# Two joined graph layers on one core: wo's last rows as one packed product, y scaled on ScalarE, and another order of root's low parts

## What is computed

```python
# layer 0 (2 relations, width 286), on norm_x = ln_weight * x * rsqrt(mean(x^2) + eps)
out = norm_x @ W_root + bias + sum_r segment_mean_r(norm_x @ W_rel[r])     # 625 x 286
y   = elu(out) @ wo_weight                                                 # 286 x 1024
x1  = layernorm(x + (x + y))
# layer 1 (8 relations, width 1024)
u   = x1 @ root + bias + sum_r segment_mean_r(x1) @ weight[r]
z   = concat([u, x1]) @ w_gate + b_gate
h   = tanh(u) * z + x1 * (1 - z)
return layernorm(x1 + h)
```

## Time and profile before

| | us |
|---|---|
| median of 3 runs (838.40 to 838.87) | 838.75 |
| the profiled execution's own time | 838.58 |
| its span | 836.8 |
| TensorE busy | 818.8 |
| VectorE (DVE) busy | 671.8 |
| ACT busy | 438.3 |

### The profile page before, as it was taken

How to read it: one execution, slowest core, us unless ns; L and a number is a source line. 1 busy time by engine, 2 the same in 40 slices (tenths; PEclk the granted TensorE clock), 3 DMA queues, 4 the chain that set the end, 5 groups by cost and what they waited for, 6 DMA issues and landing times.

```text
span 836.8 us, 15905 instructions
## 1 busy us (share of the span) xinstructions
PE 818.8 (98%) x6326; PEld 586.4 (70%) x6326; DVE 671.8 (80%) x969; ACT 438.3 (52%) x606; POOL 14.4 (2%) x32
## 2 busy tenths in 40 slices
PE   7999999999999999999999999999999999999996
PEld 6566744468876868768677686786867868768544
DVE  8999698998978677687776777767778677788996
ACT  6888568376555354453554535535446254445711
POOL 1000000000000000000000000000000000000000
PEclk9999999999999999999999999999999999999998
DMA  9512369202220220202202112022020220305711
GB/s 316 114 26 27 131 224 227 101 1 101 102 101 1 101 102 1 100 15 85 100 0 100 44 56 100 0 100 71 29 100 0 100 100 2 127 1 151 201 51 73
DMA packets 60124, 70.82 MB, mean 85 GB/s; under 512 B 30662, under 2 KB 34370, under 8 KB 60083
## 3 DMA queue, kind: packets, MB, share of 16 engines
q1 hardware_dynamic: 59207, 69.39, 26.3%
q10 hardware_dynamic: 876, 0.85, 0.4%
HBM read 57.71 MB, written 5.18 MB: 75 GB/s over the span
## 4 chain that ended last, share of the span: by engine, by line
PE 88%; DVE 7%; ACT 3%; issue 1%; DMA 1%; SPq 0%; DVEq 0%; ACTq 0%
PE psP L1162 51%; PE psA L1233 21%; PE psP L982 12%; PE psA L971 2%; PE psP L1086 1%; PE psP L942 1%; ACT cu_mem L676 1%; DVE p_mem L1463 1%; DVE vec L1384 1%; ACT wsplit L709 1%; DVE p_mem L1462 1%; ACT dump L596 0%; DMA stage<-in_src 0%; DVE wsplit L1410 0%; DMA xT<-cu_mem 0%
## 5 line engine op out<-in xcount | busy, mean ns | idle before, releaser
L1162 PE MATMUL psP<-wsplit,xT 128*128 128x256 f16 x2592 | 294.6, 273 | 0.0
L1162 PEld LDWEIGHTS psP<-wsplit,xT 128*128 128x128 f16 x2592 | 253.6, 98 | 33.0
L1233 PE MATMUL psA<-p_mem,cu_mem 128*128 128x512 f16 x800 | 175.3, 379 | 0.0
L1162 PE MATMUL psP<-wsplit,x 128*128 128x256 f16 x1296 | 150.3, 273 | 0.0
L1233 PEld LDWEIGHTS psA<-p_mem,cu_mem 128*128 (+1 forms) x800 | 78.2, 98 | 91.1 <-DVE cu_mem L1722 0.3
L1162 PEld LDWEIGHTS psP<-wsplit,x 128*128 128x128 f16 x1296 | 126.8, 98 | 14.7
L1424 DVE SCALAR_TENSOR_TENSOR wsplit<-stage,sc,wsplit 128x1024 f16<-128x1024 f32 x90 | 114.8, 1279 | 26.8 <-ACT wsplit L671 26.8
L671 ACT ACTIVATE wsplit<-stage,sc 128x1024 f16<-128x1024 f32 x90 | 100.6, 1137 | 16.6 <-DVE sc L1302 10.6
L1722 DVE SCALAR_TENSOR_TENSOR cu_mem<-psA,coef,cu_mem 128x512 f32<-128x512 f32 x80 | 60.0, 750 | 31.3 <-PE psA L1233 29.9
L671 ACT ACTIVATE wsplit<-x,sc 128x1024 f16<-128x1024 f32 x54 | 61.7, 1143 | 41.6 <-PE psP L1162 31.0
L1424 DVE SCALAR_TENSOR_TENSOR wsplit<-x,sc,wsplit 128x1024 f16<-128x1024 f32 x54 | 69.2, 1282 | 10.2 <-ACT wsplit L671 9.8
(11 more groups left out here) (207 smaller groups left out, 792.5 us busy)
## 6 DMA issues: line engine op xcount, KB each, us to landing
stage<-in_L_gnn_weight SPq DMA_DIRECT2D x16, 2048.0 KB, 7.7
stage<-in_L_gnn_w_gate SPq DMA_DIRECT2D x4, 2048.0 KB, 8.2
x_home<-x SPq DMA_DIRECT2D x5, 512.0 KB, 3.8
x<-x_home SPq DMA_DIRECT2D x5, 512.0 KB, 5.5
x<-in_x SPq DMA_DIRECT2D x4, 512.0 KB, 8.6
xT<-in_L_gnn_root SPq DMA_DIRECT2D x1, 2048.0 KB, 8.9
stage<-in_L_gnn_root SPq DMA_DIRECT2D x1, 2048.0 KB, 8.4
out<-x SPq DMA_DIRECT2D x4, 512.0 KB
```

The lines of the kernel that those rows point to most:

```text
L1162: last = nc.tensor.matmul(psP[:, bank, (col + tt) * FB:(col + tt + 1) * FB], lhs[tt](a, c), split_block(n, b)[:, c, :], start=(first and t ...
L1233: last = nc.tensor.matmul(psA[:, (NT * h + t) % 2, :], cnt8[:, r, s, t * P:(t + 1) * P], p_part[h][a][:, s, :], start=(s == 0 and a == 0), ...
```

## The change

- wo's last 30 rows are loaded three times, at partitions 0, 32 and 64 of the last chunk. y's last 30 columns are also written three times, so that after the turn partitions 0 to 29, 32 to 61 and 64 to 93 of the last chunk hold them. wo's rows at partitions 32 to 63 are replaced by their low part, y's columns at partitions 64 to 95 by theirs. One matmul over 96 partitions then gives all three products (`packed_product`), 7 matmuls instead of 9 per half tile.
- `wo_high` and `wo_low` go chunk by chunk, `wo_low` right behind `first_sums` on DVE and no longer behind `agg0_add(3)`; `unit_scale(U_WO)` goes ahead of the last `first_sums`. TensorE asks for the last `q_done` only at the ninth matmul of the aggregates.
- y is scaled on ACT (`y_scaled`: two activations with a scale and a bias a tile), with the bias from one tiny DVE operation (`y_shift`). The parts of root's `weight_sum` and of `raw_high(U_ROOT)` are placed anew around it.
- `y_low` becomes two operations, 256 columns on all partitions and 128 columns on partitions 64 to 95.
- All four low parts of root's first half come before the first `wo_add`. `y_high(4)` comes behind the first deviation on ACT.
- `aggregate0(4)` goes ahead of `turn_y(0)` and `turn_y(1)`. wo's products 7 and 8 go to the two banks of `psA`, 9 to bank 2 of `psP`, and root's products 2 to 4 wait for all ten adds of wo.

```diff
@@ sync
-            sp.dma_start(st_wo[0:F - (FC - 1) * P, FC - 1, :], wo_d[(FC - 1) * P:F, :]).then_inc(wo_tail_loaded, 16)
+            for q in range(3):
+                sp.dma_start(st_wo[q * QUAD:q * QUAD + FREST, FC - 1, :], wo_d[(FC - 1) * P:F, :]).then_inc(wo_tail_loaded, 16)
-            sp.wait_ge(wo_lo, 1)
+            sp.wait_ge(wo_lo, FC)
             load(U_ROOT + 1, 1, by_chunk(root_d[:, HALF:D]))
@@ scalar
+            def y_scaled(t):
+                act.wait_ge(y_factors, 1 if t < 2 else 2)
+                last = elu_tmp[:, t, F - FREST:F].unsqueeze(1).broadcast_to([P, 2, FREST])
+                twice = acc0[:, t, F - FREST + QUAD:F - FREST + 3 * QUAD].rearrange("p (q f) -> p q f", q=2)[:, :, 0:FREST]
+                nc.scalar.activation(twice, last, ACT.Identity, bias=y_shift[:, t:t + 1], scale=rows_f[:, 0, 2, t:t + 1])
+                nc.scalar.activation(acc0[:, t, 0:F], elu_tmp[:, t, :], ACT.Identity, bias=y_shift[:, t:t + 1],
+                                     scale=rows_f[:, 0, 2, t:t + 1]).then_inc(y_ready, 1)
-            for t in range(NT - 1):
-                elu_exponential(t)
-            y_high(0)
-            y_high(1)
-            weight_sum(U_ROOT, 0, slot_load(U_ROOT), parts=(0, 1))
-            elu_exponential(NT - 1)
-            weight_sum(U_ROOT, 0, slot_load(U_ROOT), parts=(2, 3))
+            elu_exponential(0)
+            elu_exponential(1)
+            weight_sum(U_ROOT, 0, slot_load(U_ROOT), parts=(0,))
+            y_scaled(0)
+            y_scaled(1)
+            weight_sum(U_ROOT, 0, slot_load(U_ROOT), parts=(1, 2, 3))
+            elu_exponential(2)
+            elu_exponential(3)
+            y_high(0)
+            elu_exponential(NT - 1)
+            y_high(1)
+            raw_high(U_ROOT, 0, (0, 1, 2))
+            for t in range(2, NT):
+                y_scaled(t)
             y_high(2)
             y_high(3)
-            raw_high(U_ROOT, 0)
-            y_high(4)
+            raw_high(U_ROOT, 0, (3,))
...
             for t in range(NT):
                 ln_deviation(0, t)
+                if t == 0:
+                    y_high(NT - 1)
                 x1_apply(t)
@@ tensor
+            def packed_product(out, t, cols):
+                _, hi, lo = unit_weights(U_WO)
+                for c in range(FC - 1):
+                    for a, w, first in ((0, hi, c == 0), (0, lo, False), (1, hi, False)):
+                        nc.tensor.matmul(out, yT[:, a, c, bass.ts(t, P)], w[:, c, cols], start=first, stop=False)
+                return nc.tensor.matmul(out, yT[0:3 * QUAD, 0, FC - 1, bass.ts(t, P)], hi[0:3 * QUAD, FC - 1, cols],
+                                        start=False, stop=True)
-                pe.wait_ge(wo_added, NT + t + 1)
+                pe.wait_ge(wo_added, NT + t + 1 if t < 2 else 2 * NT)
+            WO_FREE = {NT: (wo_added, 1), NT + 1: (wo_added, 2), NT + 2: (y_lo, 4), NT + 3: (y_lo, 5), NT + 4: (wo_added, 3)}
@@ vector
+            def wo_low(c):
+                st, hi, lo = (v[:, c, :] for v in unit_weights(U_WO))
+                if c == FC - 1:
+                    st, hi, lo = (v[QUAD:2 * QUAD, :] for v in (st, hi, hi))
+                dve.wait_ge(wo_hi, c + 1)
+                scale = sc_f[QUAD:2 * QUAD, scale_col(U_WO, 1), 2:3] if c == FC - 1 else sc_f[:, scale_col(U_WO, 1), 2:3]
+                stt(lo, st, scale, hi, ALU.mult, ALU.subtract).then_inc(wo_lo, 1)
...
+            unit_scale(U_WO, 1)
             dve.wait_ge(flag_ready, 1)
...
             first_sums(NT - 1, 1)
...
-            unit_scale(U_WO, 1)
+            for c in range(FC):
+                wo_low(c)
...
+            def y_factor(t0, t1):
+                tiles = slice(t0, t1)
                 dve.wait_ge(elu_done, t1)
+                step(nc.vector.tensor_reduce(rowmax[:, 0, tiles], elu_tmp[:, tiles, :], AX.X, ALU.max))
+                row_scales([rows[:, 0, a, tiles] for a in range(4)], rowmax[:, 0, tiles].bitcast(I32), least=127)
+                ts(y_shift[:, tiles], rows_f[:, 0, 2, tiles], -1.0, None, ALU.mult).then_inc(y_factors, 1)
+                ts(cy[:, tiles], rows_f[:, 0, 3, tiles], sc_f[:, U_WO, 3:4], 0.5, ALU.mult, ALU.mult).then_inc(cy_ready, 1)
             def y_low(t):
                 dve.wait_ge(y_hi, t + 1)
+                nodes, third = slice(t * P, (t + 1) * P), slice(2 * QUAD, 3 * QUAD)
+                tt(yT[:, 1, 0:FC - 1, nodes], psA[:, t % 2, 0:FPAD - P].rearrange("p (c n) -> p c n", c=FC - 1),
+                   yT[:, 0, 0:FC - 1, nodes], ALU.subtract)
+                tt(yT[third, 0, FC - 1, nodes], psA[third, t % 2, FPAD - P:FPAD], yT[third, 0, FC - 1, nodes],
+                   ALU.subtract).then_inc(y_lo, 1)
             agg0_add(0)
             agg0_add(1)
-            elu_end(0, 2)
+            elu_end(0)
+            elu_end(1)
+            y_factor(0, 2)
             agg0_add(2)
             agg0_add(3)
-            wo_low()
+            agg0_add(4)
+            unit_scale(U_ROOT, 0)
             y_low(0)
+            for t in range(2, NT):
+                elu_end(t)
+            y_factor(2, NT)
             y_low(1)
-            agg0_add(4)
-            elu_end(2, NT)
-            unit_scale(U_ROOT, 0)
+            raw_low(U_ROOT, 0, (0,))
             y_low(2)
             y_low(3)
+            raw_low(U_ROOT, 0, (1, 2, 3))
...
             wo_add(0, 0)
             wo_add(0, 1)
-            raw_low(U_ROOT, 0, (0, 1))
+            y_low(4)
             x1_factors(0)
-            y_low(4)
             wo_add(1, 0)
+            wo_add(1, 1)
             x1_low(0)
-            wo_add(1, 1)
-            raw_low(U_ROOT, 0, (2, 3))
             x1_factors(1)
```

More of the change, by code:

```diff
@@ L333, in build @@
         elu_done = sem("elu_done")
+        y_factors = sem("y_factors")
         cy_ready = sem("cy_ready")
@@ L632, in wo_high @@
                 act.wait_ge(w_used, 1)
[L633 to L634 removed]
+                st, hi, _ = unit_weights(U_WO)
+                for c in range(FC):
+                    nc.scalar.activation(hi[:, c, :], st[:, c, :], ACT.Copy,
+                                         scale=sc_f[:, scale_col(U_WO, 1), 2:3]).then_inc(wo_hi, 1)
             def weight_sum(i, slot, loads, parts=range(4)):
@@ L651, in weight_sum, with raw_high @@
                                          accum_out=am[:, slot, n:n + 1]).then_inc(wsum_ready, 1)
-            def raw_high(i, slot):
+            def raw_high(i, slot, blocks=range(4)):
                 act.wait_ge(scale_step, 4 * i + 4)
-                for n, (k, f) in enumerate(RAW):
+                for n in blocks:
+                    k, f = RAW[n]
                     b = weight_blocks(i) + n
@@ L963, in count_any, with product @@
                             quad(b, q0 + p, False)
-            def product(out, lhs, i, t, cols, part=None):
+            def product(out, lhs, i, t, cols, part):
                 _, hi, lo = unit_weights(i)
-                chunks = FC if i == U_WO else DC
-                for c in part or range(chunks):
+                for c in part:
                     for a, w, first in ((0, hi, c == 0), (0, lo, False), (1, hi, False)):
                         last = nc.tensor.matmul(out, lhs[:, a, c, bass.ts(t, P)], w[:, c, cols],
-                                                start=first, stop=(c == chunks - 1 and a == 1))
+                                                start=first, stop=(c == DC - 1 and a == 1))
                 return last
+            def packed_product(out, t, cols):
[5 more added lines that the diff above has]
+                                        start=False, stop=True)
             def raw_product(out, lhs, i, t):
@@ L1076, in _ @@
                 pe.wait_ge(any_copied, BANKS + 2)
-            pe.wait_ge(q_done, 3 * NT + 3)
+            pe.wait_ge(q_done, 3 * NT)
             def aggregate0(t):
@@ L1084, in aggregate0 @@
                     for s in range(NT):
+                        if n == 0 and s == NT - 1:
+                            pe.wait_ge(q_done, 3 * NT + 3)
                         for a in range(2):
@@ L1094, in turn_y @@
                     pe.wait_ge(y_lo, t - 1)
-                for c in range(FC):
-                    last = nc.tensor.transpose(psA[:, t % 2, c * P:(c + 1) * P], acc0[:, t, c * P:(c + 1) * P], ident[:, :])
-                last.then_inc(y_turned, 1)
+                for c in range(FC - 1):
+                    nc.tensor.transpose(psA[:, t % 2, c * P:(c + 1) * P], acc0[:, t, c * P:(c + 1) * P], ident[:, :])
+                nc.tensor.transpose(psA[0:3 * QUAD, t % 2, (FC - 1) * P:FPAD],
+                                    acc0[:, t, (FC - 1) * P:(FC - 1) * P + 3 * QUAD], ident[:, :]).then_inc(y_turned, 1)
+            WO_FREE = {NT: (wo_added, 1), NT + 1: (wo_added, 2), NT + 2: (y_lo, 4), NT + 3: (y_lo, 5), NT + 4: (wo_added, 3)}
             def wo_product(t):
                 if t == 0:
-                    pe.wait_ge(wo_hi, 1)
-                    pe.wait_ge(wo_lo, 1)
```

(23 more changed lines are left out.)

19 lines of the change are left out of this document (8 added, 11 removed).

## The result

The kernel after took 840.83 us (median of seven executions, 839.11 to 841.81), the kernel before 838.75 beside it (838.40 to 839.54): ratio 1.0024, interval 1.0014 to 1.0033. The forecast was 838.8 with a range from 836.8 to 840.5, so the result lies 0.33 above its upper end.

The account below looks back on a forecast made before the run. The prediction took root's first product start, held by the order of work on DVE and ACT, as the bound. Root 0.1 us later on 838.58, with the median 0.17 above that run, gave 838.8; range 836.8 to 840.5.

Parts of the forecast that it names:

- The sum: Profiled run of 838.58 plus 0.1 for root's later start, median 0.17 above that run: 838.8, no change.
- Hidden parts: On TensorE, packed product saves 4 of 18 matmuls per tile, 4.3 us in all, worth nothing as TensorE waits.
- Rival (c): Slower: TensorE's longer pauses drop its clock at root's start, one tile at 1.2 GHz costs 5.2 us, 844; chance 0.03.
- Steps 1, 2 and 5: DVE and ACT lines: wo_low ends 91.8; y scaling moves to ACT, second y_factors 107.85; x1_low(0) ends 125.5, 124.24 before.
- Step 3: On DVE, y_low's two pieces don't overlap: 0.77 a tile against 0.46; with overlap 0.93 less in all.
- rival (d): The forecast itself: DVE has as much to do as before, -0.8 to +1.1, 838.0 to 839.9; chance 0.77.
- Step 4: ACT's scaling of y puts y_high(2) at 111.0, DVE idles some 1.2 us; called the step that eats the gain.
- Step 6: SP issues x1's low rows at 125.55, landing 3.1 to 3.4 later; root starts about 128.95, 0.1 later.
- (a): Faster: DVE pieces overlap, small ACT operation and third low part are cheap; root starts 126.9, time 836.8; chance 0.14.
- (b): Slower: earlier load of root's second half delays the first half up to 5 us; landing 99.4 gives 841.9; chance 0.06.

Follow-up runs that it names:

- wo_19_matmuls: Kernel after with three matmuls into unused columns behind each half of wo's product, 4.9 us of TensorE in all: 840.10 us, ratio 1.0017.
- fill14: Kernel after with 14 matmuls into unused columns in TensorE's pause ahead of root: 839.55 us, ratio 1.0011.
- before_fill3: Kernel before with 3 matmuls into unused columns ahead of root, a control: 838.84 us, ratio 0.9998.
- before_short3: Kernel before, last degree matmuls moved ahead of tile 4's product, which leaves out both low parts (3 matmuls a half): 841.54 us, ratio 1.0030.
- fill8_nohold: Kernel after with 8 matmuls into unused columns ahead of root, second y_low and third wo_low pieces on all 128 partitions: 838.25 us, ratio 0.9994.
- fill12_yscale_dve: Kernel after with 12 matmuls into unused columns ahead of root, y scaled on DVE again: 839.99 us, ratio 1.0018.
- after_fill_early: Kernel after with 12 matmuls into unused columns ahead of tile 2's second half, none ahead of root: 841.50 us, ratio 1.0028.
- after_fill4: Kernel after with 4 matmuls into unused columns ahead of root: 839.75 us, ratio 1.0015.
- before_short6: Kernel before, last degree matmuls moved ahead of tile 4's product, which leaves out y's low part (6 matmuls a half): 839.68 us, ratio 1.0012.
- yhigh4_nofill: Kernel after with y_high(4) ahead of the first deviation on ACT, no matmuls added in the pause: 840.38 us, ratio 1.0013.

## Why the prediction failed

**The step that failed is the clock.** The sum took the root's 240 matmuls at 51.96 and TensorE's pauses as free. "Hidden parts" booked the packed product as "nothing" because TensorE already waited. But less work on an engine that waits is more pause, and here the pause had a price. The pause grew by 1.9 us: counted from the ten small matmuls ahead of the aggregates, TensorE is done 1.3 earlier (126.68 − 84.94 against 128.29 − 85.24) and the root starts 0.6 later. In wo_19_matmuls, with the saved work put back, the pause is 0.29. Rival (c) had the mechanism and the place, and with 2.4 us even the pause, but a chance of 0.03 and a price of 5.2 us for one whole tile. The runs show it in most executions, at 1.48 us in the kernel after and up to 2.83 in other kernels, since the clock came back sooner than after a tile (in the kernel after within the window from 132 to 133). This is shown by fill14 (with filler the root takes 51.96 again, starts where it did, and 1.14 us come back), before_fill3 (filler alone does nothing) and before_short3 (the clock falls without any part of the change, and the root takes 2.83 more). The argument against (c) was that the granted clock was 1.00 from 109 to 129; that row holds no pause as long as the new one, so it could not speak against it.

**Steps 1, 2 and 5** held within 0.4 us: `wo_low` ends at 91.48 (91.8 forecast), `y_shift` starts at 97.10 (97.4 for the factors' end, 97.27 measured), 107.40 plus 0.17 for the second (107.85), `y_high(2)` released DVE at 110.65 (111.0), low part 3 at 115.85 (near 116), `x1_low(0)` at 125.41 (125.5). ACT's small operation took 0.44 and 0.42, the pair 0.86 against 0.87.

**Step 3** was right on the mechanism. Its size without the changes of partition was forecast at 0.93 for the path; fill8_nohold measured 1.46 against the kernel after. The forecast was too low by its own terms: four tiles at 0.24 are 0.96 already, and the third `wo_low` (0.21) comes on top. It also left out that the operations behind the pieces are held, such as the first add of wo (0.1). In the same way, rival (d)'s upper end of +1.1 is lower than the +1.6 and +0.5 that it names as its bounds; neither came, as the pieces took 0.42 and 0.29 and the small ACT operation 0.44.

**Step 4** was right on the wait (0.88 against 1.2) and wrong to name it as what eats the gain; with the scaling back on DVE (fill12_yscale_dve) the root starts 0.39 later.

**Step 6** was 0.15 off: the low rows landed after 3.54 us, beyond the median of 3.4.

Without the clock the forecast of +0.1 was still a little low. Root − aggregate is 43.45 (mean of the kernel after, fill14, after_fill_early and after_fill4) against 42.17 (mean of the six profiles of the kernel before and its variants), 1.28 later, and the aggregate starts 0.66 earlier, where the forecast had 0.8. So the root starts 0.6 later. fill14's median is 0.94 above the kernel before, with an interval from 0.2 to 1.7 us, which holds 0.6; whether anything is missing between them is not shown. Rivals (a) and (b) fell: nothing new was cheap, and root's first half landed after 9.1 us beside the second load, 8.9 without it.

What stays open is when exactly the clock falls. The pause's length is not all of it: 2.10 us in before_short6 kept the clock in the profiled execution and 1.58 in yhigh4_nofill lost it. The moment differs, too: within the pause in the kernel after, behind the root's first matmuls in yhigh4_nofill, in the wait before the last one in before_short3. The table suggests that another wait of over a microsecond shortly before makes a fall likelier, but after_fill_early took the earlier one away and lost the clock all the same.

## What to carry to other kernels

An engine that waits is not free to wait longer if it is TensorE: after each change, compare its longest pauses ahead of dense matmuls with the longest that the trace has shown at full clock, and look at how long the matmuls behind them take. Where the pause grows past those, a few matmuls into unused PSUM columns are a cheap test, and in this kernel also the cure (1.14 and 1.72 us in the medians). Splitting an operation on VectorE costs by its start partition too: keep pieces that start elsewhere together, since each change cost about 0.1 us here.

## What was new about the hardware

The clock fell to its lower level in a pause of 2.42 us in the kernel after, and in some executions of yhigh4_nofill just behind one of 1.58 us. In the kernel after it stayed there for some 3 us of dense matmuls (129 to 132) before it rose; in after_fill_early, where the root took 54.77, it stayed for longer. The Trainium skill, page "TensorE: Matmul & The Clock Gate", section "HAM oscillation — how this bites in real kernels", warns of longer idle gaps than these; here shorter ones were enough, in most executions, so the measurement decides. Whether it falls differs between executions of one program: two groups of times 2 us apart in yhigh4_nofill. With light work between two pauses (before_short3: three matmuls in 1.46 us behind a wait of 1.48) the clock was down in the profile from 125 to 133 us, from the first of the two on, and all six times lay between 841.18 and 841.70.
